# Identity first, slots turned earlier, biases spread on ScalarE, and half of the own rows scaled on ScalarE in two of three GAT passes

## The reference

```
h = relu(layernorm(x));  x = x + GAT(h)
h = relu(layernorm(x));  x = x + NET(h)

GAT, three layers (each node has a loop to itself):
  h = x @ W;  s = h @ a_src;  d = h @ a_dst
  e = leaky_relu(s[src] + d[dst], 0.2)
  alpha = softmax of e over the edges with one destination
  x = x + sigmoid(sum over dst of alpha * h[src] + b)

NET, three layers:
  e   = relu([x[src], x[dst], e_before] @ We + be)
  agg = sum over dst of e * norm
  x   = relu([x, agg] @ Wn + bn)
```

## Time and profile before

| engine | busy us | share of the span |
|---|---|---|
| TensorE | 5078.0 | 84% |
| VectorE | 4339.4 | 72% |
| ScalarE | 3405.6 | 57% |
| GpSimd | 3537.2 | 59% |

### The profile page before, as it was taken

The page is one execution under the profiler, slowest core; times in us unless marked ns, Lnnn a source line. Parts: engine busy times, 40 slices in busy tenths (PEclk is TensorE's granted clock), DMA queues, the critical chain, the costliest instruction groups (busy, mean ns, idle before and its releaser), DMA issues. The chain is left out here.

```text
span 6014.0 us, 100399 instructions
## 1 busy us (share of the span) xinstructions
PE 5078.0 (84%) x23996; PEld 3008.8 (50%) x23996; DVE 4339.4 (72%) x11924; ACT 3405.6 (57%) x7493; POOL 3537.2 (59%) x3533
## 2 busy tenths in 40 slices
PE   4999999999994768847884888799989997777775
PEld 2666666666652235424442444466656664333332
DVE  7988888888874899958885999566645555544453
ACT  4888888888874956735663577533323333222222
POOL 3544444444421657437764775277767765777777
PEclk9999999999997977967886999899999999999998
DMA  9999997777655857736664899677667774444442
GB/s 218 308 302 299 303 299 240 244 244 238 230 189 168 290 172 214 206 118 187 203 198 128 265 294 284 204 219 218 215 210 234 234 220 146 133 130 130 132 131 80
DMA packets 909508, 1274.03 MB, mean 212 GB/s; under 512 B 248502, under 2 KB 398967, under 8 KB 902579
## 3 DMA queue, kind: packets, MB, share of 16 engines
q1 hardware_dynamic: 696170, 1063.92, 54.0%
q0 software_dynamic: 112896, 202.19, 13.9%
q10 hardware_dynamic: 100016, 3.20, 1.3%
HBM read 623.49 MB, written 654.07 MB: 212 GB/s over the span
## 5 line engine op out<-in xcount | busy, mean ns | idle before, releaser
L1738 POOL DMA_INDIRECT n_xs<-table,look x1176 | 1197.8, 1019 | 558.8 <-issue 349.8
L1439 POOL DMA_INDIRECT g_xs<-table,look x784 | 775.8, 989 | 454.1 <-issue 233.6
L1877 DVE TENSOR_TENSOR_SCAN n_dT<-n_km,n_dT,bank 128x512 f32<-128x512 uint8 x291 | 372.3, 1279 | 496.1 <-PE bank L1765 493.3
L626 POOL DMA_INDIRECT p_rows<-in_x_dram,dst_ix x392 | 390.4, 996 | 487.5 <-DMA raw_rows<-p_rows 264.7
L634 POOL DMA_INDIRECT table<-slot_pair,map_ix x392 | 397.1, 1013 | 454.5 <-ACT n_sg L742 247.7
L670 PE MATMUL bank<-n_xT,gat_w 128*128 128x512 f32 (+1 forms) x1176 | 545.2, 599 | 18.4 <-ACT n_xT L734 16.3
L689 PE MATMUL bank<-n_zT,wn 128*128 128x512 f32 (+1 forms) x1176 | 537.1, 592 | 6.6 <-ACT n_zT L734 6.6
L1750 POOL DMA_INDIRECT out_dram<-n_xn,n_row_of x392 | 385.5, 983 | 140.0 <-issue 118.5
L1557 ACT ACTIVATE g_xw<-g_xs,g_cols 128x128 f32<-128x128 f32 x1176 | 370.7, 387 | 76.1 <-PE bank L1507 49.0
L1859 ACT ACTIVATE n_xn<-bank 128x512 f32<-128x512 f32 x98 | 58.4, 596 | 624.8 <-DMA out_dram<-n_xn,n_row_of 624.8
L865 DVE COPY n_ro<-bank 128x512 f32<-128x512 f32 (+1 forms) x392 | 256.4, 685 | 197.3 <-PE bank L699 134.4
(11 more groups left out here) (278 smaller groups left out, 12574.7 us busy)
## 6 DMA issues: line engine op xcount, KB each, us to landing
table<-n_ro SPq DMA_DIRECT2D x768, 256.0 KB
g_gb<-decays SPq DMA_DIRECT2D x294, 256.0 KB
n_xd<-table SPq DMA_DIRECT2D x294, 256.0 KB
table<-g_xn SPq DMA_DIRECT2D x196, 256.0 KB
g_xo<-table SPq DMA_DIRECT2D x196, 256.0 KB
edge_feats<-n_eT SPq DMA_DIRECT2D x196, 256.0 KB
table<-n_xn SPq DMA_DIRECT2D x196, 256.0 KB
n_ea<-edge_feats SPq DMA_DIRECT2D x196, 256.0 KB
```

The lines of the kernel that those rows point to most:

```text
L626: q.indirect_dma_start(out=edge_rows[e % UX][:, u, :], out_offset=None, in_=x, in_offset=bass.IndirectOffsetOnAxis(ap=dst_ix[:, t:t + 1], ...
L1439: q.indirect_dma_start(out=xs[g % XR][:, u, :], out_offset=None, in_=tables[l], in_offset=bass.IndirectOffsetOnAxis(ap=src_ix[:, t:t + 1] ...
L1738: q.indirect_dma_start(out=xs.buffers[g % UE][:, u, :], out_offset=None, in_=tables[L], in_offset=bass.IndirectOffsetOnAxis(ap=look[:, t, ...
L1877: V.tensor_tensor_scan(in_order(dT[g][:, :]), kept(g), in_order(flat_banks[1]), 0.0 if begins(g) else carry(dT[g.before(1)]), ALU.mult, AL ...
```

## The change

In setup the identity has a semaphore of its own and is loaded second, ahead of the edge arrays. TensorE turns `slots` and `wcol` before the products of the constants. VectorE splits the biases before the records, and ScalarE, which waits for the identity and for these steps, writes `brow3` and `brow7`. In the first and third GAT pass (`UA` = 2) ScalarE also multiplies the own rows of tiles 2 and 3 by their weights into a new ring `so` of 2; VectorE keeps the multiply-add for tiles 0 and 1 and adds `so` to the other two in one instruction of 128x256. ScalarE's part waits for the own rows and for the add of two groups before. In all three passes `load_own` goes from lag 15 to lag 14.

```diff
-            consts = [(ident[:, :], eye), (gat_w[:, :, :], gat_w_in), (wT[:, :, :], gat_wt_in),
+            consts = [(gat_w[:, :, :], gat_w_in), (wT[:, :, :], gat_wt_in),
...
+                    v.wait_ge(s_cl, 16 * len(consts))
+                    do(V.tensor_copy(part[0][:, :, :], bias_rows[:, :, :]))
...
+                    mark["bias"] = n[0]
                     do(V.tensor_tensor(tmp[:, 0, :], f_dst, f_nxt, ALU.not_equal))
...
-                    v.wait_ge(s_cl, 16 * len(consts))
-                    do(V.tensor_copy(part[0][:, :, :], bias_rows[:, :, :]))
...
-                    for l in range(LAYERS):
-                        do(V.tensor_copy(brow3[l][:, :, :], brest[:, l:l + 1, :].broadcast_to([3, U, C])))
-                        for u in range(U):
-                            do(V.tensor_copy(brow7[l][:, u, :], ident[0:3 + U, 3 + u:4 + u].broadcast_to([3 + U, C])))
-                        seen()
-                        do(V.tensor_copy(brow7[l][0:3, :, :], brest[:, LAYERS + l:LAYERS + l + 1, :]
-                                         .broadcast_to([3, U, C])))
...
                 @block.tensor
                 def _(pe):
+                    pe.wait_ge(s_ey, 16)
+                    pe.wait_ge(s_el, 16 * len(edge_loads))
+                    for of, k in ((slots, 2), (wcol, 3)):
+                        for u in range(U):
+                            last = T.transpose(banks[k][0:GE, u, :], of[:, u:NT:U], ident[:, :])
+                        last.then_inc(s_tr, 1)
                     pe.wait_ge(s_cl, 16 * len(consts))
...
-                    pe.wait_ge(s_el, 16 * len(edge_loads))
-                    for of, k in ((slots, 2), (wcol, 3)):
-                        for u in range(U):
-                            last = T.transpose(banks[k][0:GE, u, :], of[:, u:NT:U], ident[:, :])
-                        last.then_inc(s_tr, 1)
...
+                @block.scalar
+                def _(a):
+                    a.wait_ge(s_ey, 16)
+                    for l in range(LAYERS):
+                        for u in range(U):
+                            last = S.activation(brow7[l][:, u, :], ident[0:3 + U, 3 + u:4 + u].broadcast_to([3 + U, C]), ACT.Copy)
+                    last.then_inc(s_bp, 1)
+                    a.wait_ge(s_bp, 1)
+                    a.wait_ge(s_dv, mark["bias"])
+                    for l in range(LAYERS):
+                        S.activation(brow3[l][:, :, :], brest[:, l:l + 1, :].broadcast_to([3, U, C]), ACT.Copy)
+                        S.activation(brow7[l][0:3, :, :], brest[:, LAYERS + l:LAYERS + l + 1, :].broadcast_to([3, U, C]), ACT.Copy)
...
                     sp.dma_start(first_numbers[:, :], node_numbers).then_inc(s_nl, 16)
+                    sp.dma_start(ident[:, :], eye).then_inc(s_ey, 16)
...
+            UA = 0 if l == 1 else 2
...
+                so = of_ring(f"g{l}_so", 2, (P, UA, P), c=c2) if UA else None
...
-                            for u in range(U):
+                            for u in range(U - UA):
                                 last = V.scalar_tensor_tensor(out=xw[g % 3][:, u, :], in0=xo[g % OR][:, u, :],
                                                               scalar=column(g, 1, u), in1=xw[g % 3][:, u, :],
                                                               op0=ALU.mult, op1=ALU.add)
+                            if UA:
+                                last = V.tensor_tensor(xw[g % 3][:, U - UA:U, :], xw[g % 3][:, U - UA:U, :], so[g % 2][:, :, :],
+                                                       ALU.add)
...
-                                  (9, store_decays), (17, load_decays), (15, load_own)]
+                                  (9, store_decays), (17, load_decays), (14, load_own)]
...
                                 last = S.activation(xw[g % 3][:, u, :], xs[g % XR][:, u, 0:C], ACT.Copy, scale=column(g, 0, u))
+                            if UA:
+                                landed(a, ol, g)
+                                ready(a, selfed, g - 1)
+                            for u in range(U - UA, U):
+                                last = S.activation(so[g % 2][:, u - U + UA, :], xo[g % OR][:, u, :], ACT.Copy,
+                                                    scale=column(g, 1, u))
                             last.then_inc(scaled, 1)
```

More of the change, by code:

```diff
@@ L237, in build @@
         s_cl = sem("constants_loaded")
+        s_ey = sem("identity_loaded")
+        s_bp = sem("bias_copied")
         s_el = sem("edges_loaded")
@@ L369, in _ @@
                     mark["first_slots"] = n[0]
+                    v.wait_ge(s_cl, 16 * len(consts))
+                    do(V.tensor_copy(part[0][:, :, :], bias_rows[:, :, :]))
+                    seen()
+                    do(V.tensor_tensor(brest[:, :, :], bias_rows[:, :, :], part[0][:, :, :], ALU.subtract))
+                    seen()
+                    do(V.tensor_copy(part[1][:, :, :], brest[:, :, :]))
+                    seen()
+                    do(V.tensor_tensor(brest[:, :, :], brest[:, :, :], part[1][:, :, :], ALU.subtract))
+                    seen()
+                    do(V.tensor_copy(part[2][:, :, :], brest[:, :, :]))
+                    seen()
+                    do(V.tensor_scalar(brest[:, :, :], part[0][:, :, :], ident[0:3, 0:1], None, ALU.mult))
+                    for k in (1, 2):
+                        seen()
+                        do(V.scalar_tensor_tensor(out=brest[:, :, :], in0=part[k][:, :, :], scalar=ident[0:3, k:k + 1],
+                                                  in1=brest[:, :, :], op0=ALU.mult, op1=ALU.add))
+                    seen()
+                    mark["bias"] = n[0]
                     do(V.tensor_tensor(tmp[:, 0, :], f_dst, f_nxt, ALU.not_equal))
```

## The result

| kernel | median of runs, us | profiled execution, us | its span, us | mean clock |
|---|---|---|---|---|
| before | 6016.97 (8 runs) | 6015.73 | 6014.0 | 0.928 |
| after | 6000.75 (8 runs) | 6003.55 | 6001.8 | 0.931 |

The ratio of the times is 0.9968, 95% interval 0.9958 to 0.9979: faster by 0.32%, some 19 us by the ratio, 16.2 by the medians. One of the eight runs after took 12775 us and stands alone; the other seven lie between 5997.67 and 6003.55. The forecast was 6000.0.

A forecast was written before the change was run, and what follows sets the result against it. VectorE was taken to set the first and third GAT pass, gathers the second. Terms 0 - 2.6 + 0 - 13.2 = -15.8 brought 6015.73 us to 5999.9, 6000 as a median; range 5982 to 6020.

The forecast's parts named there:

- what takes its place is the SyncE queue: Setup: VectorE's chain ends near 38.3 us, but SyncE's last store still lands at 52.3; change 0.
- The relief per group: VectorE in a changed GAT group: two multiply-adds replaced by one plain add of 0.34 us, saving 0.19 us.
- The forecast cycle: Third pass: seven groups take 36.9 us, with TensorE, VectorE and ScalarE busy 33, 36 and 31.
- The step of early cycles: First pass, nine early cycles of seven groups: ScalarE's later rows nearly cancel VectorE's saving, -0.15 us each, about -1.
- the whole relief arrives: Rival, chance 0.16: early first-pass cycles run at the higher clock like late ones, 16 us more saved, 5985 us.
- it is idle for little of it: First pass, early cycles: ScalarE idles only 0.15 us of its 3.38 us step, so the step grows by 0.45.
- Late cycles: First pass, four cycles late in it: scaled rows are ready some 3 us early, so -1.3 us each, -5.2.
- The drain: End of the first pass, gathers over: VectorE isn't the bound, ScalarE's step grows 0.45 us over eight steps, +3.6.
- The forecast of ten to twenty microseconds of VectorE's waits for ScalarE: First pass: more than ten waits of VectorE for ScalarE, 10 to 20 us in all in place of 4.0.
- The slower rival: Rival, chance 0.12: in the first pass TensorE runs one step more per cycle at its lower clock, 6039 us.
- my own bound of 2 us: Second pass: the prediction would be wrong if this pass changed by more than 2 us.

The follow-up runs named there:

- the zeros moved: Five stores of zeros moved from setup into the node pass: kernel before 6016.18 us, 0.9998; changed kernel with the add as multiply-add 5989.28 us, 0.9950.
- the other form of the add: Changed kernel with its plain add of 128x256 written as a multiply-add with the constant 1.0: 5997.93 us, 0.9959 to the kernel before.
- ScalarE's part alone: Changed kernel, but VectorE does all four multiply-adds and nobody reads what ScalarE scales into `so`: 6018.04 us, 1.0002 to the kernel before.
- VectorE's alone: Changed kernel, but VectorE adds own rows of tiles 2 and 3 unweighted and ScalarE scales nothing more: 5993.87 us, 0.9959 to the kernel before.

## Why the prediction was right, and where it wasn't

**Setup: right (0; measured +0.2).** The step "what takes its place is the SyncE queue" is shown from both sides: one chain removed changes nothing, the other removed changes nothing, both removed give 7 us.

**The relief per group: right.** The add lasts 0.41 us and the next instruction starts 0.33 behind it (forecast 0.40 to 0.45 and 0.34).

**Third pass: right.** Forecast -13.2. The two profiles alone show -10.7. Five kernels with this pass as before took 634.8, 635.7, 637.1, 637.1 and 637.4 us (mean 636.4), five with ScalarE's half and an add of either form 624.1, 622.1, 623.9, 622.1 and 624.4 (mean 623.3): -13.1. The forecast cycle is met. One step of it was off: the room between the last gather and VectorE was to shrink from 33 us to 20, and shrank to 10 (columns as in the earlier trace rows), because the gathers of this pass became slower as well (mean 0.998 us between 3240 and 3830, 0.966 before).

```profile
L1455 POOL DMA_INDIRECT g_xs<-table,look x784: 941/947/2047, 2614.3 to 3729.5; - x196
L1281 DVE CUSTOM_DVE_ANT_0 g_junk<-g_xs,v_src x1176: 252/276/358, 2130.3 to 3739.7; 128x128 f32<-128x128 f32 x196
```

They don't set the pass yet.

**First pass: wrong (-2.6; measured -9.6, and -8.6 between the means of five unchanged passes, 504.2, and five changed ones, 495.7).** Unchanged are the kernel before, setup, load and third pass alone, and the zeros moved; changed are the changed kernel, the first pass alone, all three, the other form of the add, and that with the zeros moved. Two steps failed, with opposite signs.

*The step of early cycles, -0.15 each.* It took TensorE's steps at the lower clock as given and let ScalarE's 0.6 us add to them. In fact the whole relief arrived in them. The start of the running sum of the fifth group, and every seventh from there, give the cycles of the pass (the filling first, the end of the drain last), in us:

```
before  58.6 | 33.1 33.2 34.3 33.9 34.0 34.1 34.1 34.1 33.5 | 33.2 33.1 30.9 22.2 | 23.5
after   57.2 | 31.9 31.9 32.6 31.9 32.5 31.9 31.9 31.9 32.0 | 32.6 37.8 32.4 25.3 | 22.7
```

The filling gives -1.4, the nine full cycles -16.0 where about -2.5 was forecast (eight early ones at -0.15, the first late one at -1.3), the next four +8.7 and the end -0.8. In five kernels with an unchanged first pass the nine take 300.7 to 306.2 us, in five changed ones 287.0 to 288.4: 15.6 less between the means. That is the 1.3 of the relief nine times and some 0.4 more in each. Unchanged passes have cycles of 33.1 and of 34.1 us, the longer mostly at a clock of 0.80; changed ones nearly all take 31.9. So most of what the lower clock had cost went away too. That is the mechanism of my rival "the whole relief arrives", to which I had given 0.16 with the argument that a longer ScalarE step makes TensorE wait more.

ScalarE's part alone refutes the argument. The step that failed is "it is idle for little of it": in the first pass ScalarE waited for TensorE for over 120 us, and most of its new work went into these waits. Its two largest waits for TensorE, before and after (columns as in the earlier trace rows):

```profile
ACT g_nT L1590 <- PE bank L1538: 76.5, 54, 4.2
ACT g_dt L1595 <- PE bank L1544: 43.5, 89, 1.2
```
```profile
ACT g_nT L1612 <- PE bank L1554: 44.1, 36, 2.8
ACT g_dt L1617 <- PE bank L1560: 27.6, 44, 1.2
```

They fell by 48.3 us while ScalarE's busy time grew by 49.3 (331.1 to 380.3); with ScalarE's part alone they fell by 44.0. The clock over the nine cycles is 0.82 to 0.87 in the five unchanged kernels, 0.90 with ScalarE's part alone (299.6 us), 0.91 with VectorE's alone, and 0.91 to 0.95 in the five changed ones. So the whole change raises it. That ScalarE's part does so by itself rests on one trace that lies just outside the unchanged ones, and why more is granted isn't shown.

*Late cycles, -1.3 each.* They were to follow VectorE, but there the gathers decide now. In the earlier trace rows GpSimd issued 26 or 27 gathers in a cycle while one needs 28, so VectorE was slowly catching up with it; with cycles of 31.9 it issues 22 or 23, and VectorE meets it at 2503. The last gather starts at 2537.6 (2491.1 before), and this takes most of the 8.7 us. Before, 131 us lay between the last gather's start and the end of the pass, now 76. I had checked that room for the third pass and not for the first.

*The drain, +3.6.* ScalarE is busy 25.30 of 25.30 us there and its step went from 3.38 to 3.71, +0.33 in place of +0.45. The sign was right; over eight steps that is 2.6. This is where ScalarE's part shows: the cycle that takes 22.2 us before and 22.4 with VectorE's part alone takes 25.1 with ScalarE's part alone and 25.3 after.

The forecast of ten to twenty microseconds of VectorE's waits for ScalarE was wrong too: 6.8, since ScalarE had its own waits to take the work from. The slower rival needed more steps at the lower clock; the clock of the pass rose.

**Second pass: right (0), though by my own bound of 2 us the +4.8 should have refuted it.** The bound was wrong: the thirteen kernels in which nobody edits that pass's instructions scatter over 11.5 us.

**Sum.** The two terms as the means of five kernels each have them add up to -8.6 - 13.1 = -21.7. The medians say -16.2, and the ratio's interval, -12.6 to -25.3 us of 6017, holds both. In the one pair of profiles the untouched passes gave back 8 us (+0.2 + 2.5 - 1.4 + 4.8 + 1.9), so the forecast of -15.8 is in part lucky: it looks more exact than its terms were. By the ratios the third pass alone gives 0.28% and the first 0.04 to 0.08%, less than the 0.14% of its 8.6 us, but inside the intervals.

## What to carry to other kernels

Where two chains end a stage, take out both or neither: either alone measures as nothing. When an engine that paces a pass is made faster, ask of every feeder how far ahead it is and how much longer it can stay so; a feeder off the path in the profile before can be the bound after. And before a bound is set on a stage's change in one profile, look at how that stage scatters between kernels that don't differ in it.

## What was not expected of the hardware

- GpSimd's gathers can fall into step with VectorE's rhythm. In steps of 3.56 us they took 1.20 and 1.75 us in turn, beside a plain add of 0.41 and a two-source instruction of 0.65, where they take 0.94 undisturbed. The 264 gathers of the pass went from 263.7 to 307.8 us.
- Whether the two-source instruction of 0.65 us holds a gather depends on where the gather starts: from 0.25 us ahead of its start to 0.35 behind, 1.60 us on average; 0.3 to 1.0 us ahead of it, 0.95 at most.
- The granted clock over nine cycles rose from 0.82 to 0.87 in unchanged first passes to 0.91 to 0.95 in changed ones, though ScalarE had more to do. In the long cycle, in which VectorE waits for gathers, it is 0.77 here but 0.91 in four of the other kernels with VectorE's part, so no rule follows from the 0.77.
